# Moving the loads of x, context and residual behind the stacks in SyncE's queue

## The reference

```
x = layernorm(x + self_attention(x))          # 16 heads of 16, rotary q and k, softmax over 256 keys
x = layernorm(x + cross_attention(x, ctx))    # 120 keys; two softmaxes over 8 dims each, a1 - lam * a2
x = layernorm(x + experts(x) + shared(x))     # 64 experts, top 6, capacity 96; shared MLP of 512

# self:  q, k, v = x @ qkv_w + qkv_b;  q, k = rotary(q), rotary(k)
#        softmax(q k^T / 4) v, then @ out_w + out_b
# cross: q from x, k and v from ctx;  softmax(q1 k1^T * s) - lam * softmax(q2 k2^T * s), times v
```

## Time and profile before

| | |
|---|---|
| median of 3 runs | 1912.32 us (1907.93 to 1921.76) |
| the profiled execution | 1915.7 us, span of the instructions 1913.6 us |
| mean granted clock of PE | 0.947 |
| busy PE / DVE / ACT / POOL | 88% / 68% / 57% / 45% of the span |
| mean DMA rate | 158 GB/s |
| self stage, steady (103 to 690 us) | 587 us, PE busy 556.53 |
| cross stage, steady (887 to 1439 us) | 552 us, PE busy 499.04 |

### The profile page before, as it was taken

How to read it: one execution, slowest core, us unless ns; L and a number is a source line. 1 busy time by engine, 2 the same in 40 slices (tenths; PEclk the granted TensorE clock), 3 DMA queues, 4 the chain that set the end, 5 groups by cost and what they waited for, 6 DMA issues and landing times. The chain is left out here.

```text
span 1913.6 us, 43700 instructions
## 1 busy us (share of the span) xinstructions
PE 1682.0 (88%) x14562; PEld 1186.9 (62%) x14562; DVE 1296.3 (68%) x2959; ACT 1082.9 (57%) x1701; POOL 858.1 (45%) x788
## 2 busy tenths in 40 slices
PE   3799999999999998889989889989898749999985
PEld 2566666666676665556556556655554438888774
DVE  3566777666766776668888878878887444443275
ACT  1466666666666665667777767767775401111244
POOL 4566777676767752212121112211121005787565
PEclk7899999999999999899999999999998759999998
DMA  5577767777678775466655666666654227887696
GB/s 122 126 199 175 195 176 184 190 190 180 166 194 192 189 175 145 118 127 135 137 133 131 139 125 143 140 127 130 129 125 92 79 62 184 193 200 195 175 293 218
DMA packets 312751, 302.79 MB, mean 158 GB/s; under 512 B 68842, under 2 KB 289836, under 8 KB 303304
## 3 DMA queue, kind: packets, MB, share of 16 engines
q1 hardware_dynamic: 302408, 288.66, 61.6%
q0 software_dynamic: 10240, 12.81, 3.9%
HBM read 188.36 MB, written 112.00 MB: 157 GB/s over the span
## 5 line engine op out<-in xcount | busy, mean ns | idle before, releaser
L1344 DVE TENSOR_REDUCE att_nmax<-self_p_mx 128x2 f32<-128x512 f32 x512 | 328.8, 687 | 201.6 <-PE self_p_mx L633 201.2
L1434 DVE TENSOR_REDUCE att_cross_nmax<-self_p_mx 128x8 f32<-128x960 f32 x256 | 294.9, 1152 | 93.6 <-PE self_p_mx L833 92.7
L1078 ACT ACTIVATE att_probs<-self_p_sc 128x1024 f32<-128x1024 f32 x256 | 261.2, 1020 | 94.5 <-PE self_p_sc L621 92.5
L1171 ACT ACTIVATE att_probs<-self_p_sc 120x1024 f32<-120x1024 f32 x256 | 261.9, 1023 | 65.9 <-PE self_p_sc L815 65.1
L633 PE MATMUL self_p_mx<-att_k_stack,att_q_stack 96*128 96x256 bf16 x1024 | 161.9, 278 | 54.1 <-DMA att_k_stack<-self_k_parts 48.5
L851 PE MATMUL self_p_pv<-att_probs,att_v_aug 120*32 120x256 f32 x2048 | 171.9, 409 | 0.0
L621 PE MATMUL self_p_sc<-att_q_stack,att_k_stack 99*128 99x256 bf16 x1024 | 158.0, 277 | 11.6 <-ACT att_probs L1078 10.0
L833 PE MATMUL self_p_mx<-att_k_stack,att_q_stack 48*128 48x120 bf16 x2048 | 100.7, 219 | 69.3 <-DMA att_k_stack<-cross_k_parts 44.2
L1695 POOL TENSOR_SCALAR att_cross_var_eps<-att_cross_mv 128x2 f32<-128x2 f32 x32 | 7.2, 226 | 329.0 <-DVE att_cross_mv L1544 289.4
L633 PEld LDWEIGHTS self_p_mx<-att_k_stack,att_q_stack 96*128 96x128 bf16 x1024 | 96.0, 99 | 83.4 <-DMA att_k_stack<-self_k_parts 37.0
L1709 POOL TENSOR_TENSOR att_qk_rest<-att_qk,att_parts 128x752 f32<-128x752 f32 x32 | 51.8, 1620 | 213.4 <-ACT att_parts L1204 213.4
(11 more groups left out here) (180 smaller groups left out, 3641.6 us busy)
## 6 DMA issues: line engine op xcount, KB each, us to landing
att_q_stack<-self_q_parts SPq DMA_DIRECT2D x64, 256.0 KB, 5.8
expert_sums<-att_zeros SPq DMA_DIRECT2D x64, 256.0 KB, 8.6
att_q_stack<-cross_q_parts SPq DMA_DIRECT2D x128, 128.0 KB
ffn_w<-in_ffn_w SPq DMA_DIRECT2D x64, 256.0 KB
ffn_m_sb<-expert_sums SPq DMA_DIRECT2D x32, 512.0 KB, 5.8
self_q_parts<-att_parts SPq DMA_DIRECT2D x32, 384.0 KB
self_k_parts<-att_parts SPq DMA_DIRECT2D x32, 384.0 KB
att_k_stack<-self_k_parts SPq DMA_DIRECT2D x32, 384.0 KB, 7.8
```

Of the source, the lines that this page charges most:

```text
L1078: act.activation(probs[:, g % 4, :], p_sc[:, :, :].rearrange("p b n -> p (b n)"), ACT.Exp, scale=SCALE).then_inc(s_exp, 1)
L1171: act.activation(probs[0:KEYS, g % 4, :], p_sc[0:KEYS, :, :].rearrange("p b n -> p (b n)"), ACT.Exp, scale=C_SCALE).then_inc(c_exp, 1)
L1344: dve.tensor_reduce(nmax[:, M.slot, :, m], p_mx[:, m % 2, :].rearrange("p (c k) -> p c k", c=TC), AX_X, ALU.max, negate=True).then_inc(s_r ...
L1434: dve.tensor_reduce(cnmax[:, M.slot, :, :, 2 * m:2 * m + 2].rearrange("p c e h -> p e h c"), p_mx[:, :, 0:4 * KEYS].rearrange("p e (x k) - ...
```

## The change

In the first piece of SP's step the order is changed. Self stage: the stack loads of B come first, with their waits, and the loads of xT and x_res after them. Cross stage: the stack loads of B come first, then the wait for their landing (now whenever B is on, no longer only when R is on too), and only then the loads of x, context and residual, and then the stores. No instruction is added or removed in the steady steps; the loads, their waits and sizes are the same.

```
@@ self step, first piece @@
                 X, A, B, M, S, O, R = (at_lag(lag) for lag in range(7))
-                if X.on:
-
-                    if past(X.n, 3):
-                        sp.wait_ge(s_vp, X.n - 2)
-                    sp.dma_start(xT[:, X.slot, :, :], xT_rows[X.n]).then_inc(s_x[X.slot], 16)
-                    if opens(X):
-                        other_loads()
-                if S.on:
-
-                    if past(S.n, 3):
-                        sp.wait_ge(s_sum, S.n - 2)
-                    sp.dma_start(x_res[:, S.slot, :, :], x_rows[S.n]).then_inc(s_res_in[S.slot], 16)
                 if B.on:
...
                         sp.dma_start(stack[row:row + m, B.slot, :], src[src_row:src_row + m, :])\
                           .then_inc(s_st[B.slot], 16)
+                if X.on:
...
+                if S.on:
...
                 if R.on:
                     sp.wait_ge(s_yb, R.n + 1)
@@ cross step, first piece @@
+                if B.on:
+                    n_pw = held(sp, 64 * (B.turn + 1))
+                    sp.wait_ge(c_wts, 16)
+                    sp.wait_ge(c_pw[B.slot], n_pw)
...
+                            sp.dma_start(stack[e * HALF + row:e * HALF + row + m, B.slot, 0:NH * n],
+                                         src[src_row:src_row + m, :]).then_inc(c_st[B.slot], 16)
+                if B.on:
+                    n_st = held(sp, 16 * C_N_ST * (B.turn + 1))
+                    sp.wait_ge(c_wts, 16)
+                    sp.wait_ge(c_st[B.slot], n_st)
                 if X.on:
...
                     sp.dma_start(x_res[:, S.slot, :, :], cres_rows[S.n]).then_inc(c_res_in[S.slot], 16)
-                if B.on:
-                    n_pw = held(sp, 64 * (B.turn + 1))
...
                 if R.on:
-                    if B.on:
-                        n_st = held(sp, 16 * C_N_ST * (B.turn + 1))
-                        sp.wait_ge(c_wts, 16)
-                        sp.wait_ge(c_st[B.slot], n_st)
                     sp.wait_ge(c_y, R.n + 1)
```

More of the change, by code:

```diff
@@ L470, in step @@
                           .then_inc(s_st[B.slot], 16)
+                if X.on:
+                    if past(X.n, 3):
+                        sp.wait_ge(s_vp, X.n - 2)
+                    sp.dma_start(xT[:, X.slot, :, :], xT_rows[X.n]).then_inc(s_x[X.slot], 16)
+                    if opens(X):
+                        other_loads()
+                if S.on:
+                    if past(S.n, 3):
+                        sp.wait_ge(s_sum, S.n - 2)
+                    sp.dma_start(x_res[:, S.slot, :, :], x_rows[S.n]).then_inc(s_res_in[S.slot], 16)
                 if R.on:
@@ L518, in cross_step @@
                     counts_ahead()
+                if B.on:
+                    n_pw = held(sp, 64 * (B.turn + 1))
+                    sp.wait_ge(c_wts, 16)
+                    sp.wait_ge(c_pw[B.slot], n_pw)
+                    if not past(B.n, 3):
+                        sp.wait_ge(c_ones, B.n + 1)
+                    if past(B.n, 3):
+                        sp.wait_ge(c_sc, NGR * (B.n - 2))
+                    for e in range(E):
+                        q_src = cq_dram[B.slot][e].rearrange("t (d h) n -> (t d) (h n)", h=NH)
+                        k_src = ck_dram[B.slot][e].rearrange("t (d h) n -> (t d) (h n)", h=NH)
+                        for is_q, row, src_row, m in C_STACK_LOADS:
+                            stack, src, n = (q_stack, q_src, T) if is_q else (k_stack, k_src, KEYS)
+                            sp.dma_start(stack[e * HALF + row:e * HALF + row + m, B.slot, 0:NH * n],
[4 more added lines that the diff above has]
+                    sp.wait_ge(c_st[B.slot], n_st)
                 if X.on:
```

## The result

| | before | changed |
|---|---|---|
| median on the same chip | 1917.1 us (7 runs, 1906.31 to 1925.03) | 1929.92 us (7 runs, 1926.01 to 1930.4) |
| ratio, 95% interval | | 1.007 [1.0038, 1.0101] |
| the profiled execution | 1915.7 us, span 1913.6 | 1930.4 us, span 1928.3 |
| mean granted clock of PE | 0.947 | 0.943 |

The change makes the kernel 0.7% slower; 0.8% faster was forecast. The two profiled executions are 14.7 us apart.

What follows compares the result with a forecast made beforehand. PE's wait for the stacks' landing was taken as the bound. Self -10 and cross -5 (-19 + 14) took the profiled 1915.7 us to 1901, and 3.4 us less for the median gave 1897 us, range 1866 to 1930.

Steps and rivals of the forecast that it cites:

- slower: the tail on SP: Rival: cross stacks land no sooner, so loads issued behind the landing cost +14 to 24 us; 1934 us, chance 0.15.
- What bounds the kernel: Both attention stages: PE waits for the stacks' landing, 48.5 us self, 44.2 us cross; SP's queue order sets cross time.
- What leaves the front (cross): Cross stage: moving 632 KB from before the stack loads gains 0.7 us in 27 steps, -19 us.
- The start 0.3 us sooner: Cross stage: with three issues gone from the front, the stack loads start 0.3 us sooner a step.
- For the landing of the stacks ... I take 0.4: Cross stage: with 632 KB gone from the front, the stacks land 0.4 us sooner; 0 held as possible.
- the time from the first stack load to the landing (13.6 us in the earlier trace): Cross-stage sign: a fall by more than 0.4 us would show the front was priced too low.
- What comes at the back (cross): Cross stage: three loads behind the landing delay L573 and the parts by 0.85 to 0.9 us in 17 steps, +14 us.
- The cross part in sum: Cross stage: -19 us from the front and +14 us from the back, together -5 us.
- The self loop: Self stage: stacks land 0.9 us sooner without xT and x_res in front, half counting per step; -10 us.
- Cost 0 for the rows of the maxima: Cross stage: maxima's rows issued 0.9 us later still arrive in time; PE waits up to 1 us if not.
- The rule of the Trainium skill: Cross stage, set against the change: issue a DMA early, wait late, so the loads' old place is better; no size given.
- its first rival (1865 us): Rival, both stages: all moved bytes were in the stacks' way; self -18, cross -29 us; chance 0.2.

Runs made afterwards that it cites:

- e2: Kernel before with only the cross part of the change, self stage as before: 1936.49 us, ratio 1.0131.
- e5: Kernel before with the cross part of the change, its moved x, ctx and x_res loads cut to 16 of 128 partitions: 1924.94 us beside 1912.62.
- e4: Kernel before with the cross loads of x, ctx and x_res cut to 16 of 128 partitions, at their old place: 1913.53 us beside 1912.2.
- e12: Kernel before with the self part of the change, and the cross stores of gates and counts moved behind the stack loads: 1880.73 us, ratio 0.982.
- e1: Kernel before with only the self part of the change, cross stage as before: 1907.17 us, ratio 0.997.
- e11: Kernel before with the cross stack loads of the two partition halves issued in turn: 1891.47 us beside 1915.68.
- e7: Kernel before with the cross stacks read from the parts of another batch, two batches older: 1911.9 us beside 1912.62.
- e6: e4 with three tiny loads added between the wait for the parts and the cross stack loads: 1950.24 us beside 1912.62.
- e13: e11 with e4's cut loads in front: 1890.62 us beside 1910.46.
- e14: The changed kernel with the cross stack loads of the two halves in turn: 1900.32 us beside 1910.46.
- e3: The changed kernel with the three cross loads right behind the stack loads, ahead of the wait for their landing: 1943.56 us, ratio 1.0172.
- e10: Kernel before with the three cross loads right behind the stack loads, ahead of the landing wait, cut to 16 partitions: 1927.2 us beside 1915.68.
- e9: e4 with three 256 KB loads added between the wait for the parts and the cross stack loads: 1946.86 us beside 1915.68.

## Why the prediction was wrong

The forecast was 1897 us (1866 to 1930); the kernel took 1929.92 beside 1917.1, at the very end of the range and slower instead of faster. The rival "slower: the tail on SP", 1934 us at a chance of 0.15, is what happened in the cross stage, by its own mechanism: the front gained less than 0.5 us a step, and the tail stood alone. Its size is that of e2 (24 us); in the whole change some 5 us of self gain stand against it.

- **What bounds the kernel: right.** The wait for the stacks is what moves in every run, and SP's order sets the cross pace (e5 against e4, e12 against e1).
- **What leaves the front (cross), -19 us: this step failed.** It had two terms. The start 0.3 us sooner was right in sign and too small (0.7 against before, 0.4 against e1); the 2.7 us of the step in the earlier trace rows stand at the low end of this kernel's steps, whose mean is 3.02. "For the landing of the stacks ... I take 0.4" was wrong in sign: 13.08 us against 12.32 after the first load. The two cancel: from the parts' issue to the landing it is 15.41 against 15.34 and 15.05, a loss of 0.1 to 0.4 us a step in place of a gain of 0.7. The bound of 0 was named, "no row shows it in this stage", but no bound below zero. The 0.4 was carried over from the self stage, whose seven loads are of 128 to 384 KB; the cross stage's fourteen of 30 to 128 KB behave differently (e4 with fewer bytes, e11 with another order). The sign that was to test it would have misled: "the time from the first stack load to the landing (13.6 us in the earlier trace rows)" was one step at the high end of 11.0 to 13.8. The step of the changed kernel shown above has 13.07, which reads as a gain of over half a microsecond, while the mean rose from 12.32 to 13.08.
- **What comes at the back (cross), +14 us: right.** L573 comes 2.95 us after the landing, as forecast (2.9), against 2.40 and 2.27: 0.55 to 0.68 us in 27 steps is 15 to 18 us. A further 0.1 us a step appeared between L573 and the parts (3.36 against 3.25), about 3 us; it is absent in e5, which has the same order with few bytes, so it seems to go with the bytes.
- **The cross part in sum:** 0.72 us a step (23.06 to 23.78) is 19 us, and against e1's pace 1.15 is 31; e2 measured 24. Forecast was -5.
- **The self loop, -10 us: right mechanism, half the size.** The stacks land 0.5 us sooner after issue instead of 0.9. PE's steady waits fell by 10.6 us, as said, but over all traces the stage is 4.7 us shorter and e1 is 5 us faster: what PE doesn't wait for here it partly waits for elsewhere (L621 for the rows of the maxima 4.5 us in place of 1.6, L633 for VectorE 4.1 in place of 1.6, L772 for VectorE 3.7 in place of 2.0), and half a microsecond of landing over two steps is a quarter of a microsecond a step, 7 us in 28 steps.
- **Cost 0 for the rows of the maxima:** nearly. L815 waits for them 2.0 us in all, within the 1 us a step given for a lost cover; it lies beside the longer wait for the stacks.
- **The rule of the Trainium skill** that the prediction set against this part (DMA: Bandwidth & Descriptors, Rules for kernel authors: issue early, wait late) named the right direction. The runs agree: in the old place the three issues filled SP's wait for the parts but for 1.06 us; the new one leaves 1.9 us empty and puts 1.8 us (1267.56 to 1269.40) of issues behind the landing, of which 0.55 to 0.68 us reach the pace, since SP had to wait for the maxima there anyway.
- **The chances.** 0.37 on faster leaned in part on the full rate of the DMA engines in the self stage. With e4's result in the cross stage known, its first rival (1865 us) had no basis there.

What stays open: why fewer bytes in front make the stacks' packets slower and their landing 0.7 us longer, and why halves in turn shorten it by 0.6. Freshness of the parts makes no difference with the bytes in front (e7), and a later start with few bytes in front doesn't shorten the landing (e6); the order of the halves is shown to matter (e11, e13, e14, one run each); the resource isn't identified.

## What to carry to other kernels

Read the queue of the engine that issues the DMAs as you read the compute engines: find the stretches in which it waits for a landing anyway, and put there what nobody awaits; here moving two small stores (1.2 us of issues) out of the way of the parts gave 1.5% (0.982 of e12 over 0.997 of e1), and moving three loads out of such a wait and onto the path cost 1.3%. The loads that filled such a wait here cost nothing with 632 KB (e4); before counting on its bytes, measure the landing from the event that starts the loop and not from the first issue, since an earlier start can be eaten by a longer transfer.

## What the runs showed of the hardware

- Three loads (632 KB) issued 0.4 to 1.7 us after the issue of the last of 14 stack loads had ended delayed the landing of those by 1.1 us (14.30 in e3 against 13.19 in e10). The Trainium skill (DMA: Bandwidth & Descriptors, Queues, rings and completion order) says that each DMA engine consumes its descriptors in the order of the ring, but that a later one may finish its write before an earlier one. It gives no price; these runs do, and they speak against taking the order of issue as protection.
- Fewer bytes in front made the same 14 loads slower: 13.05 to 13.19 us against 12.23 to 12.57, in six kernels each. Three loads of 256 KB directly ahead brought them back to 12.41 (e9 against 13.08 in e6). The stacks' packets took longer by themselves: those of 8192 bytes 0.83 to 0.84 us against 0.71 to 0.79, those of 3840 bytes 0.47 to 0.48 against 0.35 to 0.42.
- The order of 14 loads of equal sum was worth 0.6 to 1.2 us: 11.68 against 12.32 with the loads in front, 11.86 against 13.05 without.
